# An attention stage whose side work is placed by groups of exponentials, with the gate as a tanh, finer division and the inverse norms as a power on POOL

## Chip, cores and metric

The kernel runs on one core of one Trainium2 chip, in one launch. The metric is device microseconds of one execution. The version before the change had a median of 1349.65 us over three runs.

## What is computed

Input x is [4 batches, 1024 positions, 128 features], float32. Four layers are applied one after the other, each as x = x + layer(layernorm(x)): a selective scan, a mixture of experts, the layer that this text is about, and the mixture of experts again. In the third layer (16 heads of 8 features):

```
sq, sk, sv = lin(x, Wsq), lin(x, Wsk), lin(x, Wsv)      # [T, head, 8]
g = exp(-softplus(lin(x, Wg)))                          # one gate per head = sigmoid(-lin)
M_t = g_t * M_{t-1} + k_t (outer) v_t                   # 8x8 state per head, over 1024 positions
h_t = q_t . M_t                                         # "retention" output, 128 wide
Q, K, V = lin(h, Wq), lin(h, Wk), lin(x, Wv)
Q, K = Q / max(|Q|, 1e-12), K / max(|K|, 1e-12)         # per head, 8 features
attn = softmax(Q K^T * softplus(temp));  out = lin(attn V, Wo)
```

## The kernel before

The stage `attention` (lines 1477 to 2011) runs full softmax attention for all four batches. A **tile** is 128 keys by 512 queries of one head. PE makes its scores (L1605) into PSUM (`att_s_ps`, two buffers of 3 and 2 tiles), ACT takes the exponential of a whole buffer in one instruction (L1770: groups of 3 and 2 tiles in turn, 410 groups in all) into a ring of 15 tiles (`att_prob`), and PE multiplies them with the values (L1620, into `att_o_ps`). Four tiles, one for each of four heads, are one **value step** v; there are 64 of them in a batch, 256 in all. The 410 groups split into 102, 102, 103 and 103 for the four batches.

While PE, DVE, ACT and POOL serve the attention of batch n - 1, the same engines prepare queries, keys and values of batch n. These pieces are the **guests**. They exist during the first three batches only (below: guest batches); batch 0 was prepared by earlier stages, and the fourth has no guest. All guests share one PSUM bank, `att_b_ps`, so they form one chain PE, DVE, PE, DVE. In the order of one guest batch: transpose x and take layernorm statistics; transpose the result; eight products ("make": keys, gate, queries, values, for either half of the positions); 16 units (PE product L1652, DVE outer product L1867, DVE scan L1878, POOL product L1575); two sums over heads (L1693); four projections to Q and K (L1707) with a bias (L1889), a square on POOL (L1581) and a reduction (L1894); the clip (L1898); the inverse norm; four scaled units (L1914); four transposes (L1716), each cut into two half-precision parts (L1921, L1923). SP then copies these parts (`hv_part`) into `att_q_st` and `att_k_st` for the next batch's scores.

The order of each engine is written out by hand. Every engine walks the same list of positions; PE, for each group e, issues the scores of e, then the value step whose exponentials were group e - 2 or earlier, and, only in groups that complete a value step (`closes(e)`, 5 groups of 8), the guest of that value step u. So a guest's place is counted in value steps, 64 to a batch, and DVE and POOL loop over value steps.

The gate: PE makes the product in `att_b_ps`; ACT takes its exponential straight from PSUM (L1758, at u = 13 and 17, behind the exponentials of that group), and PE's next product waits for that; DVE adds 1 (L1857) and takes the reciprocal in two pieces of 256 columns (L1862). The inverse norm: ACT takes the square root of all 256 sums (L1763, u = 53), DVE the reciprocal (L1902). ACT's square root and its exponential stand in different function tables.

The softmax division of batch n - 1 (reciprocal L1807 and product L1809, four pieces of 256 columns) runs in value steps 5, 7, 9 and 11 of the following batch, and for the last batch behind the end of the attention.

Of the kernel before, what the change touches and what calls it, by code (L numbers as in the profile page):

```python
# [112 lines left out]
def load_constants(t, whole):  # L113
# [17 lines left out]
    t.bg_neg = whole.sb("bg_neg", [P, 1])  # L131
# [7 lines left out]
    with Stage(nc, "load") as s:  # L139
# [6 lines left out]
        with nc.Block() as block:  # L146
# [36 lines left out]
            def _(dve):  # L183
# [10 lines left out]
                dve.tensor_scalar(t.bg_neg[:, :], t.col("bg"), -1.0, None, ALU.mult)  # L194
                dve.tensor_scalar(t.bsk_small[:, :], t.col("bsk"), 1.0 / WS, None, ALU.mult)
# [1281 lines left out]
def attention(t):  # L1477
# [30 lines left out]
    def guest(v):  # L1508
        n, u = divmod(v, W)
        return (n + 1, u) if n + 1 < B else (None, None)  # L1510

    def unit_at(u):
        return [w for w in range(UNITS) if 20 + 3 * w // 2 == u]

    with Stage(nc, "att") as q:
# [12 lines left out]
        ss, rn, rt = q.sb("ss", [P, 4, NT * H]), q.sb("rn", [P, 4, NT * H]), q.sb("rt", [P, 2, NT * H])  # L1528
        unit = qm[:, 0:4, :].rearrange("p i (a c) -> p i a c", c=P)
# [9 lines left out]
        inverted, normed = q.count("inverted", 4), q.count("normed", 4)  # L1539
# [5 lines left out]
        made, copied, gated = q.count("made", 8), q.count("copied", 6), q.count("gated", 2)  # L1545
        opened, gate_made = q.count("opened", 2), q.count("gate_made", 4)
# [3 lines left out]
        clipped, rooted, rn_done, scaled = (q.count(n) for n in ("clipped", "rooted", "rn_done", "scaled"))  # L1550
# [4 lines left out]
        with nc.Block() as block:  # L1555

            @block.gpsimd
            def _(pool):
                pool.memset(va[:, :, :, :, HD:32], 1.0).then_inc(blank, 1)
# [8 lines left out]
                def weigh(n, w):  # L1568
                    h, m = divmod(w, HD)
                    pool.wait_ge(scanned.sem, scanned.at(n - 1, w))  # L1570
                    if m == 0:
                        pool.wait_ge(copied.sem, copied.at(n - 1, 3 * h + 1))
# [11 lines left out]
                for v in range(V):  # L1584
                    n, u = guest(v)
                    if u in TURN_X_AT:
                        deviation(n, TURN_X_AT.index(u))
                    if u in PROJECT_QK_AT:
                        square(n, PROJECT_QK_AT.index(u))
                    for w in unit_at(u):  # L1590
                        weigh(n, w)

            @block.tensor
            def _(pe):
# [29 lines left out]
                def project(i, h):  # L1624
                    pe.wait_ge(normed.sem, normed.at(i, 2 * h + 1))
# [48 lines left out]
                def key_value(n, w):  # L1674
                    h, m = divmod(w, HD)
                    if w == 0:
                        pe.wait_ge(copied.sem, copied.at(n - 1, 5))
# [41 lines left out]
                def entertain(n, u):  # L1719
                    if u in TURN_X_AT:  # L1720
                        turn_x(n, TURN_X_AT.index(u))
                    if u in TURN_Z_AT:
                        turn_z(n, TURN_Z_AT.index(u))
                    if u in range(MAKE_AT, MAKE_AT + 8):
                        make(n, u - MAKE_AT)
                    for w in unit_at(u):
                        key_value(n, w)
                    if u in SUM_AT:
                        add_heads(n, SUM_AT.index(u))
                    if u in PROJECT_QK_AT:  # L1730
                        project_qk(n, PROJECT_QK_AT.index(u))
                    if u in TURN_QK_AT:
                        turn_qk(n, TURN_QK_AT.index(u))

                done = 0
                for e in range(GROUPS + BEHIND):
# [5 lines left out]
                    if e < GROUPS and closes(e):  # L1742
# [3 lines left out]
                        n, u = guest(v)  # L1746
                        if n:
                            entertain(n, u)
# [4 lines left out]
            def _(act):  # L1753
                act.sem_inc(exped.sem, exped.start)

                def gate(n, h):
                    act.wait_ge(made.sem, made.at(n - 1, 4 * h + 1))
                    act.activation(g_sb[:, HALVES[h]], b_ps[:, :], ACT.Exp, bias=t.col("bg"),  # L1758
                                   scale=1.0 / WS).then_inc(gated.sem, 1)

                def root(n):
                    act.wait_ge(clipped.sem, clipped.at(n - 1))
                    act.activation(rn[:, :, :], ss[:, :, :], ACT.Sqrt).then_inc(rooted.sem, 1)  # L1763

                for e in range(GROUPS):
# [6 lines left out]
                    if closes(e):  # L1772
                        n, u = guest(first // GH)
                        if u in (MAKE_AT + 2, MAKE_AT + 6):
                            gate(n, (u - MAKE_AT) // 4)
                        if u == ROOT_AT:
                            root(n)

            @block.vector
            def _(dve):  # L1780
# [20 lines left out]
                def divide(i, k):  # L1801
                    cols = slice(k * 256, (k + 1) * 256)
                    if k == 0:
                        dve.wait_ge(moved, (i + 1) * G * MOVES)
                    if k == 2:
# [64 lines left out]
                def scan(n, w):  # L1870
                    h, m = divmod(w, HD)
                    if m == 0:
                        dve.wait_ge(gate_made.sem, gate_made.at(n - 1, 2 * h + 1))
# [52 lines left out]
                def entertain(n, u):  # L1926
                    if u in TURN_X_AT:
                        statistics(n, TURN_X_AT.index(u))
                    if u in NORMAL_AT:
                        normalise(n, NORMAL_AT.index(u))  # L1930
                    if u in TURN_Z_AT:
                        take_z(n, TURN_Z_AT.index(u))
                    if u in range(MAKE_AT, MAKE_AT + 8):
# [215 lines left out]
```

## Time and profile before

| quantity | value |
|---|---|
| three runs | 1346.37, 1349.65, 1355.12 us (median 1349.65) |
| profiled execution | 1350.3 us, of which span 1348.5 us |
| mean granted TensorE clock | 0.926 |
| PE busy | 1086.2 us (81%) |
| ACT busy | 955.5 us (71%) |
| DVE busy | 815.1 us (60%) |
| POOL busy | 344.2 us (26%) |

Busy times are of the whole program; PE is the matmul array, PEld its weight loads. The attention stage reaches from about 577 to 1183 us of the span. A busy PE means that its queue held a running matmul, and in the table nothing is said of who waited for whom; that is read stage by stage.

### The profile page before, as it was taken

The numbers are of one execution on the slowest core, as the hardware profiler recorded it, in microseconds if no ns is written. First come the engines' busy times: TensorE is split into PE (matmuls) and PEld (weight loads), VectorE is DVE, ScalarE is ACT, GpSimd is POOL, SyncE is SP. The second block draws the span as 40 slices with busy tenths as digits, with TensorE's granted clock in tenths as the row PEclk, the third lists the DMA queues.
The fourth block names the chain that finished last, engine by engine and source line by source line (L and its number), as shares of the span: only waits on it lengthen the run. The fifth ranks groups of instructions, "written<-read, shape, count | busy, mean of one in ns | idle before, by whom it ended". The sixth has DMA issues, their size and how long they took to land. (4 is left out here: it accounts for less than half of the span.)

```text
span 1348.5 us, 16297 instructions
## 1 busy us (share of the span) xinstructions
PE 1086.2 (81%) x5850; PEld 384.9 (29%) x5850; DVE 815.1 (60%) x1141; ACT 955.5 (71%) x908; POOL 344.2 (26%) x230
## 2 busy tenths in 40 slices
PE   4647788777699985568997889888997888679996
PEld 3212333233344432212222212222221111134443
DVE  6679999999467747534753666345753300356664
ACT  4667656655388862167888877887878999558885
POOL 3026867668111103210330023100330000011110
PEclk9877999999799997779998999899998999879999
DMA  3001010000101100010101011010110111001112
GB/s 99 10 1 46 32 59 35 32 31 32 32 32 32 32 1 0 1 32 11 24 18 25 21 24 24 9 36 8 24 23 18 31 25 31 8 32 32 32 33 62
DMA packets 24208, 36.73 MB, mean 27 GB/s; under 512 B 7362, under 2 KB 11970, under 8 KB 24130
## 3 DMA queue, kind: packets, MB, share of 16 engines
q1 hardware_dynamic: 24130, 35.71, 9.8%
q8 instruction: 46, 0.75, 0.2%
q14 instruction: 32, 0.26, 0.1%
HBM read 16.82 MB, written 6.29 MB: 17 GB/s over the span
## 5 line engine op out<-in xcount | busy, mean ns | idle before, releaser
L1770 ACT ACTIVATE att_prob<-att_s_ps 128x1536 f32<-128x1536 f32 (+1 forms) x410 | 478.7, 1246 | 95.7 <-PE att_s_ps L1605 95.1
L1620 PE MATMUL att_o_ps<-att_prob,att_va 128*32 128x512 f32 x2048 | 281.9, 623 | 0.0
L1605 PE MATMUL att_s_ps<-att_q_st,att_k_st 32*128 32x512 f16 x1024 | 158.6, 395 | 55.9 <-ACT att_prob L1770 39.0
L734 POOL TENSOR_TENSOR scan_hc<-scan_state,scan_c_rep 128x1024 f32<-128x1024 f32 x64 | 152.5, 2400 | 69.1 <-DVE scan_state L691 68.9
L691 DVE TENSOR_TENSOR_SCAN scan_state<-scan_decay,scan_drive_ps 128x1024 f32<-128x1024 f32 x64 | 143.3, 2271 | 1.1 <-POOL scan_hc L734 1.1
L341 PE MATMUL scan_y_ps<-scan_hc,all_ident 128*128 128x512 f32 x256 | 127.6, 623 | 8.9 <-DVE scan_y_sb L710 6.5
L669 ACT ACTIVATE scan_c_rep<-scan_c_ps 128x1024 f32<-128x1024 f32 x64 | 65.4, 1022 | 83.6 <-PE scan_c_ps L341 83.5
L1605 PEld LDWEIGHTS att_s_ps<-att_q_st,att_k_st 32*128 32x128 f16 x1024 | 37.4, 91 | 285.9 <-ACT att_prob L1770 212.3
L1575 POOL TENSOR_TENSOR att_qm<-att_mem,att_q_sb 128x512 f32<-128x512 f32 x48 | 61.1, 1276 | 203.5 <-DVE att_mem L1878 184.6
L1057 DVE SCALAR_TENSOR_TENSOR ffn_hid_lo<-ffn_hid,ffn_share,ffn_hid_hi 128x1024 f16<-128x1024 f32 x64 | 81.9, 1283 | 49.3 <-ACT ffn_hid_hi L966 48.8
L684 DVE TENSOR_TENSOR scan_drive_ps<-scan_drive_ps,ssm_du_t 128x1024 f32<-128x1024 f32 x64 | 77.3, 1220 | 13.7 <-PE scan_drive_ps L341 13.6
L962 ACT ACTIVATE ffn_hid<-ffn_h_ps,ffn_be 128x1024 f32<-128x1024 f32 x64 | 71.1, 1111 | 20.0 <-PE ffn_h_ps L351 18.6
L1799 DVE COPY att_o_sb<-att_o_ps 128x512 f32<-128x512 f32 x32 | 21.4, 670 | 100.5 <-PE att_o_ps L1620 100.4
L341 PE MATMUL scan_drive_ps<-ssm_bc,ssm_sel 96*128 96x512 bf16 x128 | 41.9, 411 | 49.8 <-DVE scan_state L691 39.3
L351 PE MATMUL ffn_o_ps<-ffn_hid_hi,ffn_w_sel 128*128 128x512 f16 x256 | 75.9, 379 | 2.2 <-DVE ffn_hid_lo L1057 2.2
L966 ACT ACTIVATE ffn_hid_hi<-ffn_hid,ffn_share 128x1024 f16<-128x1024 f32 x64 | 73.5, 1149 | 5.9
L351 PE MATMUL ffn_h_ps<-ffn_z_hi,ffn_w_sel 128*128 128x512 f16 x256 | 76.2, 379 | 0.0
L665 ACT ACTIVATE scan_decay<-ssm_dt_t,all_a_neg 128x1024 f32<-128x1024 f32 x64 | 72.9, 1140 | 0.0
L836 POOL TENSOR_TENSOR ffn_veps<-ffn_mv,all_eps 128x4 f32<-128x4 f32 x16 | 5.1, 319 | 265.0 <-DVE ffn_mv L989 265.0
L847 POOL TENSOR_TENSOR all_x_t<-all_x_t,ffn_y 128x1024 f32<-128x1024 f32 x8 | 24.1, 3007 | 171.4 <-DVE ffn_y L1051 171.4
L341 PEld LDWEIGHTS scan_y_ps<-scan_hc,all_ident 128*128 128x128 f32 x256 | 49.9, 197 | 54.0 <-issue 41.7
L1057 DVE SCALAR_TENSOR_TENSOR ffn_hid_lo<-ffn_hid,all_blend,ffn_hid_hi 128x1024 f16<-128x1024 f32 x32 | 42.6, 1330 | 37.2 <-ACT ffn_hid_hi L966 36.9
(264 smaller groups left out, 1623.7 us busy)
## 6 DMA issues: line engine op xcount, KB each, us to landing
ffn_w_sel<-w_split SPq DMA_DIRECT2D x16, 512.0 KB, 3.2
w_split<-scan_w_parts SPq DMA_DIRECT2D x8, 512.0 KB, 2.9
att_q_st<-hv_part SPq DMA_DIRECT2D x64, 64.0 KB, 2.1
att_k_st<-hv_part SPq DMA_DIRECT2D x64, 64.0 KB, 2.1
ln_x_half<-in_x SPq DMA_DIRECT2D x8, 256.0 KB, 3.0
scan_w_raw<-in_w1e SPq DMA_DIRECT2D x8, 256.0 KB, 3.3
scan_w_raw<-in_w2e SPq DMA_DIRECT2D x8, 256.0 KB, 3.5
out<-store_out SPq DMA_DIRECT2D x8, 256.0 KB, 2.6
```

Source lines behind the costliest of these rows:

```text
L341: last = pe.matmul(out[:, h], w, rhs[:, h], start=start, stop=stop)
L351: last = pe.matmul(out[:, h], w, x[:, h], start=start and i == 0, stop=stop and i == len(parts) - 1)
L665: act.activation(decay[:, n % 4, :], t.dt_t[batches[b]][:, :], ACT.Exp, scale=t.a_neg[:, n:n + 1]).then_inc(decayed.sem, 1)
L684: dve.tensor_tensor(drive_ps[n % 2][:, :], drive_ps[n % 2][:, :], t.du_t[batches[b + n // NS]][:, :], ALU.mult).then_inc(driven.sem, 1)
L691: dve.tensor_tensor_scan(state[:, k % 2, :], decay[:, k % 4, :], drive_ps[k % 2][:, :], 0.0, ALU.mult, ALU.add).then_inc(scanned.sem, 1)
L734: pool.tensor_tensor(hc[:, n % 4, :], state[:, n % 2, :], c_rep[:, n % 4, :], ALU.mult).then_inc(weighed.sem, 1)
L962: act.activation(hid[:, m % 2, :], h_ps[m % 2][:, :], ACT.Gelu_apprx_tanh, bias=b1, scale=1.0 / WS).then_inc(gelued.sem, 1)
L966: act.activation(hid_hi[:, m % 3, :], hid[:, m % 2, :], ACT.Copy, scale=weight_of_expert(k)).then_inc(casted.sem, 1)
L1057: dve.scalar_tensor_tensor(hid_lo[:, m % 3, :], hid[:, m % 2, :], weight_of_expert(m % M // FC), hid_hi[:, m % 3, :], ALU.mult, ALU.subtra ...
L1605: last = pe.matmul(s_ps[e % 2][:, k, :], k_st[rows, g % 2, kc * P:(kc + 1) * P], q_st[rows, g % 2, HALVES[half]], start=True, stop=True)
L1620: last = pe.matmul(o_ps[half][32 * j:32 * j + 32, :], va[:, g % 2, kc, j, :], prob[:, (GH * v + j) % RING, :], start=kc == 0, stop=kc == K ...
L1770: act.activation(prob[:, first % RING:first % RING + k, :], s_ps[e % 2][:, 0:k, :], ACT.Exp).then_inc(exped.sem, 1)
```

## The change

1. A guest's place is counted in groups of exponentials x (102 to a batch) and no longer in value steps u (64 to a batch). Guests may stand in any group, whether it completes a value step or not. DVE and POOL loop over groups too; what belongs to the attention itself on DVE stays at `closes(e)`. All places are new.
2. The gate: DVE copies the product out of PSUM into `g_sb` (a new instruction for each half), which frees the bank; ACT takes a tanh in place in `g_sb` with scale -1/2, three groups later; DVE makes 0.5 * tanh + 0.5 of it. This is sigmoid(-y) as before. The add of 1 and the four reciprocals of a batch are gone.
3. The division of a batch is cut in eight pieces of 128 columns at value steps 5 to 12, before in four of 256 at 5, 7, 9, 11.
4. The inverse norm is one POOL instruction on 128x256, sums to the power -0.5, in place of ACT's square root and DVE's reciprocal. Its exponent comes from a new buffer, `minus_half`, set by POOL ahead of the stage. The places: clip at x = 82, power at 83, DVE's product with the temperature at 85, scaled units at 86 and 87, transposes at 88, 90, 92 and 94.

The core of the diff:

```
-    DIVIDE_AT, PROJECT_AT = (5, 7, 9, 11), (12, 14)
-    TURN_X_AT, NORMAL_AT, TURN_Z_AT = (0, 6), (2, 8), (4, 10)
-    MAKE_AT = 11
+    PIECES = 8
+    DIVIDE_AT, PROJECT_AT = range(5, 5 + PIECES), (12, 14)
+    TURN_X_AT, NORMAL_AT, TURN_Z_AT = (0, 7), (3, 10), (5, 12)
+    MAKE_AT = range(14, 30, 2)
+    GATE_AT, OPEN_AT = (19, 27), (22, 30)
     UNITS = 2 * HD
-    OPEN_AT, INVERT_AT = (16, 19), ((17, 18), (22, 25))
-    SUM_AT = (34, 45)
-    PROJECT_QK_AT = (37, 40, 47, 48)
-    REDUCE_AT = (39, 42, 49, 50)
-    ROOT_AT, RECIPROCAL_AT, UNIT_AT, TURN_QK_AT = 53, 54, (55, 55, 56, 56), (56, 57, 58, 59)
+    UNIT_AT = tuple(31 + 5 * w // 2 for w in range(10)) + (57, 59, 63, 65, 69, 71)
+    SUM_AT = (55, 75)
+    PROJECT_QK_AT = (61, 67, 77, 79)
+    REDUCE_AT = (64, 70, 80, 82)
+    ROOT_AT, RECIPROCAL_AT, SCALE_AT, TURN_QK_AT = 83, 85, (86, 86, 87, 87), (88, 90, 92, 94)
...
-    def guest(v):
-        n, u = divmod(v, W)
-        return (n + 1, u) if n + 1 < B else (None, None)
-
-    def unit_at(u):
-        return [w for w in range(UNITS) if 20 + 3 * w // 2 == u]
+    OPENING = [group_of(GH * W * n) for n in range(B)]
+
+    def guest(e):
+        n = max(i for i in range(B) if OPENING[i] <= e)
+        return (n + 1, e - OPENING[n]) if n + 1 < B else (None, None)
...
+                def root(n):
+                    pool.wait_ge(clipped.sem, clipped.at(n - 1))
+                    pool.tensor_tensor(rn[:, :, :].rearrange("p i c -> p (i c)"), ss[:, :, :].rearrange("p i c -> p (i c)"),
+                                       minus_half[:, :], ALU.pow).then_inc(rooted.sem, 1)
...
                     if p == 0:
                         pe.wait_ge(z_rest.sem, z_rest.at(n - 1, 1))
-                    elif x == 2:
-                        pe.wait_ge(gated.sem, gated.at(n - 1, h))
                     else:
-                        pe.wait_ge(copied.sem, copied.at(n - 1, {4: 2, 1: 0, 3: 1, 5: 3, 7: 4}[p]))
+                        pe.wait_ge(copied.sem, copied.at(n - 1, p - 1))
...
                 def gate(n, h):
-                    act.wait_ge(made.sem, made.at(n - 1, 4 * h + 1))
-                    act.activation(g_sb[:, HALVES[h]], b_ps[:, :], ACT.Exp, bias=t.col("bg"),
-                                   scale=1.0 / WS).then_inc(gated.sem, 1)
-
-                def root(n):
-                    act.wait_ge(clipped.sem, clipped.at(n - 1))
-                    act.activation(rn[:, :, :], ss[:, :, :], ACT.Sqrt).then_inc(rooted.sem, 1)
+                    act.wait_ge(copied.sem, copied.at(n - 1, 4 * h + 1))
+                    act.activation(g_sb[:, HALVES[h]], g_sb[:, HALVES[h]], ACT.Tanh, bias=t.bg_half[:, 0:1],
+                                   scale=-0.5 / WS).then_inc(gated.sem, 1)
...
-                    if x == 1:
-                        return
+                    elif x == 1:
+                        dve.tensor_copy(g_sb[:, HALVES[h]], b_ps[:, :]).then_inc(copied.sem, 1)
...
-                    dve.tensor_scalar(g_sb[:, HALVES[h]], g_sb[:, HALVES[h]], 1.0, None, ALU.add).then_inc(opened.sem, 1)
-
-                def invert_gate(n, h, k):
-                    dve.wait_ge(opened.sem, opened.at(n - 1, h))
-                    cols = slice(h * HALF + k * 256, h * HALF + (k + 1) * 256)
-                    dve.reciprocal(g_sb[:, cols], g_sb[:, cols]).then_inc(gate_made.sem, 1)
+                    dve.tensor_scalar(g_sb[:, HALVES[h]], g_sb[:, HALVES[h]], 0.5, 0.5, ALU.mult,
+                                      ALU.add).then_inc(opened.sem, 1)
...
                 def reciprocals(n):
                     dve.wait_ge(rooted.sem, rooted.at(n - 1))
-                    dve.reciprocal(rn[:, :, :], rn[:, :, :]).then_inc(rn_done.sem, 1)
-                    dve.wait_ge(rn_done.sem, rn_done.at(n - 1))
```

## Rows read from the trace of the kernel before

**Rows 1.** Busy time by engine, three guest batches, then the batch without guests; columns named.

```profile
core 0: us, PE busy (x) PEld busy (x) DVE busy (x) ACT busy (x) POOL busy (x), PEclk, DMA share, GB/s
584.84:737.66 152.82, 133.57 (x940) 34.49 (x943) 75.06 (x108) 124.13 (x107) 26.96 (x24) 0.94 0.09 19
737.66:892.46 154.80, 134.94 (x961) 34.74 (x964) 84.33 (x120) 124.31 (x108) 26.88 (x24) 0.97 0.10 21
892.46:1047.99 155.53, 134.96 (x963) 34.84 (x965) 84.38 (x120) 125.79 (x108) 26.89 (x24) 0.97 0.10 21
1047.99:1165.80 117.81, 102.82 (x778) 20.47 (x778) 16.16 (x21) 116.92 (x103) 0.00 (x0) 1.00 0.12 24
```

**Rows 2.** The same view, third guest batch cut at x = 14, 31, 55, 83.

```profile
909.99:940.23 30.24, 24.46 (x176) 7.02 (x180) 15.09 (x22) 21.56 (x21) 0.33 (x1) 1.00 0.03 7
940.23:972.50 32.27, 30.28 (x214) 6.60 (x216) 25.80 (x27) 28.20 (x25) 10.20 (x8) 1.00 0.12 26
972.50:1015.31 42.81, 39.22 (x296) 11.28 (x294) 23.66 (x31) 33.14 (x28) 14.28 (x12) 1.00 0.11 22
1015.31:1047.99 32.68, 24.25 (x166) 5.97 (x170) 10.74 (x16) 26.68 (x24) 0.00 (x0) 0.90 0.10 22
```

**Rows 3.** Stretches x = 14 to 31 and from 83 on, first and second guest batch.

```profile
602.70:632.60 29.90, 24.32 (x176) 6.65 (x168) 8.18 (x12) 21.72 (x20) 0.00 (x0) 0.94 0.00 1
707.90:737.66 29.76, 22.92 (x160) 5.78 (x160) 10.74 (x16) 25.12 (x23) 0.00 (x0) 0.89 0.11 24
...
754.47:785.73 31.26, 26.57 (x183) 6.93 (x175) 16.15 (x25) 21.66 (x20) 0.12 (x1) 0.95 0.02 3
860.39:892.46 32.07, 23.70 (x164) 5.78 (x160) 10.74 (x16) 25.14 (x24) 0.00 (x0) 0.89 0.10 23
```

**Rows 4.** PE's order of time at a gate: start, length, work, idle before and releaser.

```profile
924.86 0.39 PE L1652 MATMUL att_b_ps<-att_z_hi,all_ret_hi 128*128 128x512 f16 x1 [2.13 <-ACT att_g_sb L1758]
```

**Rows 5.** ACT's order of time around the square root, third guest batch.

```profile
1011.73 8.29 ACT L1770 ACTIVATE att_prob<-att_s_ps 128x1536 f32<-128x1536 f32 x7 [0.30 <-PE att_s_ps L1605]
1020.03 1.28 ACT L1763 ACT_TABLE_LOAD   x1
...
1023.06 4.62 ACT L1770 ACTIVATE att_prob<-att_s_ps 128x1024 f32<-128x1024 f32 x4
```

**Rows 6.** PE's order of time behind the same square root.

```profile
1024.13 0.39 PE L1605 MATMUL att_s_ps<-att_q_st,att_k_st 32*128 32x512 f16 x2 [2.68 <-ACT att_prob L1770]
```

**Rows 7.** Busy time by engine in the stretch behind it (columns as in rows 1).

```profile
1025.47:1034.00 8.53, 8.53 (x44) 2.12 (x45) 2.37 (x4) 5.71 (x5) 0.00 (x0) 0.60 0.00 0
```

**Rows 8.** Groups of instructions in the stage: count, busy us, mean ns, idle before.

```profile
L1862 DVE RECIPROCAL att_g_sb<-att_g_sb 128x256 f32<-128x256 f32 x12 | 20.8, 1733 | 0.0
```

**Rows 9.** The same view, POOL's instructions.

```profile
L1575 POOL TENSOR_TENSOR att_qm<-att_mem,att_q_sb 128x512 f32<-128x512 f32 x48 | 61.1, 1276 | 203.5 <-DVE att_mem L1878 184.6 <-PE att_b_ps L1693 19.0
L1565 POOL TENSOR_TENSOR att_rstd<-att_veps,all_minus_half 128x4 f32<-128x4 f32 x6 | 6.0, 1008 | 0.5
L1563 POOL TENSOR_TENSOR att_veps<-att_mv,all_eps 128x4 f32<-128x4 f32 x6 | 1.2, 200 | 117.5 <-DVE att_mv L1822 117.5
```

**Rows 10.** The last projection on PE, in order of time.

```profile
1008.88 1.16 PE L1707 MATMUL att_b_ps<-all_qk_mats,hv_h_seq 128*128 128x128 f32 x8 [0.46 <-DVE att_raw L1889]
```

**Rows 11.** DVE's order of time from the clip to the first scaled unit.

```profile
1012.95 0.29 DVE L1898 TENSOR_SCALAR att_ss<-att_ss 128x256 f32<-128x256 f32 x1
...
1023.56 0.36 DVE L1906 TENSOR_TENSOR att_rt<-att_rn,all_heat 128x64 f32<-128x64 f32 x2
1023.96 0.69 DVE L1914 TENSOR_TENSOR att_qm<-att_raw,att_rt 128x512 f32<-128x512 f32 x1
```

**Rows 12.** ACT's order of time at the start of the last stage, behind the exponentials.

```profile
1193.36 0.20 ACT L948 ACTIVATE ffn_th<-ffn_gap 1x1 f32<-1x1 f32 x1 [1.44 <-DVE ffn_gap L1015]
1193.58 1.28 ACT L962 ACT_TABLE_LOAD   x1
```

**Rows 13.** One transpose of a scaled unit on PE, in order of time.

```profile
1038.86 0.66 PE L1716 MATMUL att_b_ps<-all_ident,att_qm 128*128 128x128 f32 x4
```

More of the change, by code:

```diff
@@ L1549, in attention @@
         qk_made, raw_done, squared, sums = (q.count(n, 4) for n in ("qk_made", "raw_done", "squared", "sums"))
-        clipped, rooted, rn_done, scaled = (q.count(n) for n in ("clipped", "rooted", "rn_done", "scaled"))
+        clipped, rooted, scaled = (q.count(n) for n in ("clipped", "rooted", "scaled"))
         unit_done, qk_turned, hi_done, lo_done = (q.count(n, 4) for n in ("unit_done", "qk_turned", "hi_done", "lo_done"))
@@ L1582, in square @@
                                        ALU.mult).then_inc(squared.sem, 1)
[L1584 to L1591, printed above, removed]
+                def root(n):
+                    pool.wait_ge(clipped.sem, clipped.at(n - 1))
+                    pool.tensor_tensor(rn[:, :, :].rearrange("p i c -> p (i c)"), ss[:, :, :].rearrange("p i c -> p (i c)"),
+                                       minus_half[:, :], ALU.pow).then_inc(rooted.sem, 1)
+                for e in range(GROUPS):
+                    n, x = guest(e)
+                    if x == ROOT_AT:
+                        root(n)
+                    if x in TURN_X_AT:
+                        deviation(n, TURN_X_AT.index(x))
+                    if x in UNIT_AT:
+                        weigh(n, UNIT_AT.index(x))
+                    if x in PROJECT_QK_AT:
+                        square(n, PROJECT_QK_AT.index(x))
             @block.tensor
@@ L1717, in turn_qk, with entertain @@
                     last.then_inc(qk_turned.sem, 1)
[L1719 to L1733, printed above, removed]
+                def entertain(n, x):
+                    if x in TURN_X_AT:
+                        turn_x(n, TURN_X_AT.index(x))
+                    if x in TURN_Z_AT:
+                        turn_z(n, TURN_Z_AT.index(x))
+                    if x in MAKE_AT:
+                        make(n, MAKE_AT.index(x))
+                    if x in UNIT_AT:
+                        key_value(n, UNIT_AT.index(x))
+                    if x in SUM_AT:
+                        add_heads(n, SUM_AT.index(x))
+                    if x in PROJECT_QK_AT:
+                        project_qk(n, PROJECT_QK_AT.index(x))
+                    if x in TURN_QK_AT:
+                        turn_qk(n, TURN_QK_AT.index(x))
                 done = 0
@@ L1771, in _ @@
                                    ACT.Exp).then_inc(exped.sem, 1)
[L1772 to L1777, printed above, removed]
+                    n, x = guest(e)
+                    if x in GATE_AT:
+                        gate(n, GATE_AT.index(x))
             @block.vector
@@ L1924, in take_qk @@
                                       ALU.subtract).then_inc(lo_done.sem, 1)
[L1926 to L1933, printed above, removed]
-                        take(n, u - MAKE_AT)
-                    if u in OPEN_AT:
-                        open_gate(n, OPEN_AT.index(u))
-                    for h in range(2):
-                        if u in INVERT_AT[h]:
-                            invert_gate(n, h, INVERT_AT[h].index(u))
-                    for w in unit_at(u):
-                        outer(n, w)
-                        scan(n, w)
-                    if u in SUM_AT:
-                        take_sum(n, SUM_AT.index(u))
-                    if u in PROJECT_QK_AT:
-                        add_bias(n, PROJECT_QK_AT.index(u))
-                    if u in REDUCE_AT:
-                        reduce(n, REDUCE_AT.index(u))
-                    if u == RECIPROCAL_AT:
@@ new lines, in entertain @@
+                def entertain(n, x):
+                    if x in TURN_X_AT:
+                        statistics(n, TURN_X_AT.index(x))
+                    if x in NORMAL_AT:
+                        normalise(n, NORMAL_AT.index(x))
+                    if x in TURN_Z_AT:
+                        take_z(n, TURN_Z_AT.index(x))
+                    if x in MAKE_AT:
+                        take(n, MAKE_AT.index(x))
+                    if x in OPEN_AT:
+                        open_gate(n, OPEN_AT.index(x))
+                    if x in UNIT_AT:
+                        outer(n, UNIT_AT.index(x))
+                        scan(n, UNIT_AT.index(x))
+                    if x in SUM_AT:
+                        take_sum(n, SUM_AT.index(x))
+                    if x in PROJECT_QK_AT:
+                        add_bias(n, PROJECT_QK_AT.index(x))
+                    if x in REDUCE_AT:
+                        reduce(n, REDUCE_AT.index(x))
+                    if x == RECIPROCAL_AT:
@@ L1950, in entertain @@
                         reciprocals(n)
                     for i in range(4):
[L1952 removed]
+                        if x == SCALE_AT[i]:
                             make_unit(n, i)
[L1954 to L1955 removed]
+                    if x in TURN_QK_AT:
+                        take_qk(n, TURN_QK_AT.index(x))
                 for g in range(2):
                     take_values(g)
[L1959 to L1970 removed]
+                for e in range(GROUPS):
+                    if closes(e):
+                        v = tiles_of(e)[0] // GH
+                        if v >= KC + 2 and (v - 3) % KC == KC - 1:
+                            g, half = divmod((v - 3) // KC, 2)
+                            take_out(g, half)
+                            if half == 1 and g + 2 < B * G:
+                                take_values(g + 2)
+                        if v >= W:
+                            if v % W in DIVIDE_AT:
+                                divide(v // W - 1, DIVIDE_AT.index(v % W))
+                            if v % W in PROJECT_AT:
+                                add_out(v // W - 1, PROJECT_AT.index(v % W))
+                    n, x = guest(e)
@@ L1971, in _ @@
                     if n:
-                        entertain(n, u)
+                        entertain(n, x)
                 take_out(B * G - 1, 1)
-                for k in range(4):
+                for k in range(PIECES):
                     divide(B - 1, k)
```

43 lines of the change are left out of this document (16 added, 27 removed).

## The prediction

> **What bounds the kernel now.** All that changes lies in the attention stage, so I read it alone, cut at the first exponential of each batch [rows 1]. The fourth batch, without guests, takes 117.81 us; ACT is busy for 116.92 of them, so there ACT is the bound, at 117.81 / 103 = 1.144 us a group. PE is at 102.82 / 117.81 = 87%. The guest batches take 152.82, 154.80 and 155.53 us: 36.1, 38.1 and 37.7 us more than 102 or 103 groups at that pace. ACT falls to 81%, PE stands at 87%. What the reader is to see: guests make PE's queue late, scores come late and ACT waits. Hence a guest costs either its own work on PE, or a wait at which PE stands with the scores behind it.
>
> Cutting the third guest batch by the new positions x [rows 2] tells the two apart. From x = 31 to 55 PE is busy for 30.28 of 32.27 us, 94%, with the clock at 1.00: nothing but work. From 55 to 83 it is 92%. From 14 to 31 (products and gates) it is 24.46 of 30.24 us, 81%, for 17 groups that would take 19.4 without guests. From 83 on (root, units, transposes) it is 24.25 of 32.68 us, 74%, at a mean clock of 0.90, for 20 groups worth 22.9. These two stretches hold the waits. The two other guest batches show the same [rows 3]: 29.90 and 31.26 us, 29.76 and 32.07 us.
>
> **The products and the gate (x = 14 to 31).** At a gate PE stands still for 2.13 us until ACT has emptied the bank, behind the exponentials of that group [rows 4]; two gates in a batch. In the new order ACT reads no bank: DVE copies, PE goes on two groups later. A DVE pass over 512 columns takes 0.69 us (the scaled unit, [rows 11]), so PE finds the bank free after two groups (2.3 us), and ACT's tanh, three groups after the copy's place, finds its input. What is queued behind each wait: behind PE's wait for the copy the next scores, behind ACT's wait for it the exponentials, behind DVE's wait for the tanh, three groups on, its next take and its copies of finished output. All three have two or three groups of room. The two stalls are 4.3 us, and a guest in every second group instead of in every value step spreads the rest. I do not book both in full: I let PE reach the 94% of the next stretch. The PE work of 24.32, 26.57 and 24.46 us then takes 25.9, 28.3 and 26.1 us; against 29.90, 31.26 and 30.24 this saves 4.0, 3.0 and 4.1. The second one holds a stretch at less than full clock (0.95) that should go with the stall, 1.5 us more. Mean 4.2 us a batch. DVE loses twelve reciprocals, 20.8 us [rows 8], and gains six copies of 0.69; it is at 54% here [rows 1], so this is worth only what it takes out of the chain, which is in the 94%.
>
> **Units, sums, projections (31 to 83).** Ten units stand in 24 groups as before; I book nothing to x = 55. From 55 to 83 PE goes from 92 to 94%: 39.22 / 0.938 = 41.8 against 42.81, 1.0 us. The tightest new wait is the second sum at 75, four groups (4.6 us) behind the last unit at 71, whose PE product, outer product, scan and POOL product (1.28 [rows 9]) come to about 4 us. It may cost some tenths either way.
>
> **Square root to power (83 on).** The exponentials end at 1020.02 and start again at 1023.06: 3.04 us, of which one table load is 1.28 [rows 5]. PE waits 2.68 us for that [rows 6], and then comes what the busy shares hide: for 8.53 us from 1025.47 the granted clock is 0.60 on average [rows 7], that is mostly at 1.2 instead of 2.4 GHz. The transposes fall into that stretch. The excess over 1.144 us a group from x = 83 on is 8.0, 10.3 and 9.8 us [rows 2, 3], mean 9.4. With the root off ACT 3.1 of them go. Of the remaining 6.3 I keep 1.4 at the end of the batch, where the next scores wait for their copies, and 1.9 for four transposes of 0.66 us [rows 13], of which part fits in PE's spare 13%. So 3.0 more goes with the half clock, and the saving is 6.1 us a batch. On the table loads the Trainium skill ("ScalarE: Activation LUTs", What ACT_TABLE_LOAD costs) adds about 1.38 us of drain to each load of 1.28, so some 5.3 us for the pair; the trace shows no drain, the load starts 0.01 us after the last exponential [rows 5]. By the page the sum would be about 7 us lower; the measurement decides.
>
> **The power's own price** is the open term: POOL, 128x256. The trace has only 128x4, 1.008 us, beside 0.200 for an add of that size and 1.276 for a multiply of 128x512 [rows 9]. Lower bound: all that the power adds is paid once, and further elements cost what a multiply's do, (1.276 - 0.200) / 508 = 2.1 ns: 1.008 + 0.53 = 1.5 us. Upper bound: all of it is paid for each element, 0.202 us: 0.200 + 256 x 0.202 = 51.9 us. For the forecast I scale it like the multiply, from 4 to 256 elements 0.734 / 0.200 = 3.7 times: 3.7 us. The multiply is the one POOL operation with both sizes here, and for it nearly all of the small instruction is a fixed part. The Trainium skill ("GPSIMD Engine Reference", Performance versus the Vector engine) gives about 2.6 cycles an element for two-input work and no price for a power; by it alone the whole instruction would be under 1 us, below my lower bound, which the 1.008 us for four elements contradicts. How much is free? From the start of the last projection on PE (1008.88 [rows 10]) to the end of the clip (1013.24 [rows 11]) passed 4.4 us. That projection now stands at x = 79, the first transpose at 88: nine groups, 10.3 us, and about 0.9 for guests between. Behind the power come the temperature product and the first unit, 1.1 us (1023.56 to 1024.65 [rows 11]). 11.2 - 4.4 - 1.1 leaves 5.7 us. At 3.7 the power is hidden; the cover is those five groups. Beyond 5.7 us PE waits at the first transpose with all scores behind it, and DVE waits with its output copy behind it.
>
> **The rest.** Eight pieces of division: hidden in the batches, where shorter pieces help a little, but exposed at the very end: eight more DVE instructions. Their fixed part is between nothing and 0.18 us, the length of an instruction of 64 columns [rows 11], so 0 to 1.4 us; I take 1.0 as each also waits for the one before it. The setting of the exponent, 256 columns on POOL, is a few tenths of a microsecond ahead of the stage, while the first scores wait for their copies: nothing. The half bias is one DVE instruction of one column during loading: nothing.
>
> **Sum.** 4.2 + 1.0 + 6.1 = 11.3 us a guest batch, 33.9 for three, less 1.0: 32.9. 1350.3 - 32.9 = 1317.4 us of the profiled execution, which stood 0.65 over the median: **1317 us**. Own range 1303 to 1331: PE at 97% through the three middle stretches (about 3.3 us a batch) and no wait for copies (1.4) give 1303; half the gain of the product stretch (2.1) and transposes that keep 2.1 more give 1331.
>
> **Rivals.**
> *A, the power is long.* For: it adds 0.8 us for four elements, four times the add, and no row has it at size. Against: the multiply's fixed part. PE stalls for X - 5.7 in each guest batch, and a stalled PE falls to half clock as after the root, so the 3.0 are lost too. All gains are eaten at X = 5.7 + 11.3 - 3.0 - 0.3 (the end) = 13.7 us; it is over 1% (13.5 us, about what this measurement can tell from no change) slower from 18.2 on. The geometric mean of 3.7 and 51.9 is 13.9, which gives no change, 1350. In full (51.9) it is 46.2 + 3.0 - 11.3 = 37.9 a batch, 1463 us.
> *B, placement buys nothing.* PE has work for 135 us in each guest batch [rows 1]; waits for DVE could take the place of the waits for ACT in the one chain through the bank. Then only x = 83 on gains: 18 - 1 = 17 us, 1333. Against it: the 2.13 us waits are on ACT, which in the new order holds no bank.
> *C, the tanh brings table loads.* Two of 1.28 at each of six gates, 15.4 us, 1333. Against: in the last stage a tanh follows the exponentials with no load before it, and the load comes only for the next function [rows 12].
>
> **Chances.** Forecast 0.50; B 0.13; A between 5.7 and 18 us 0.19, beyond 0.15; C 0.03. Faster by over 1% are the forecast nearly whole, over half of B and C, and A up to about 9.2 us: 0.61. Slower by over 1% is A beyond 18: 0.17. The rest, 0.22, is within 1%. The range goes from 1303 to 1372, where A stands at about 21 us; this leaves out about 5% below and 13% above.
>
> **What the profile will show.** ACT: no table load in the stage but the first, no pause before x = 88. PE: no wait for the gate; busy share from x = 14 to 31 at about 94%, clock 1.00 behind x = 83. POOL: three powers of 128x256; under 5.7 us I am right, near 14 or more rival A. A wait of PE for DVE at the places of the copies would be B. Guest batches of about 143 us instead of 154. I am wrong if the power is long, or if the half clock has another cause than that pause.

## The result and the profile after

The changed kernel takes 1407.92 us (median of 4 runs, 1401.16 to 1409.08) against 1351.96 us for the one before: 1.041 times as long, 95% interval 1.036 to 1.046. The forecast was 1317 us in a range to 1372; the sign was wrong. The profiled execution took 1407.79 us, its span 1406.0.

First the busy times by engine in the three guest batches and the last batch, cut at the same exponentials as [rows 1].

```profile
core 0: us, PE busy (x) PEld busy (x) DVE busy (x) ACT busy (x) POOL busy (x), PEclk, DMA share, GB/s
587.99:761.00 173.01, 133.43 (x941) 34.52 (x945) 66.70 (x105) 120.66 (x105) 68.13 (x25) 0.86 0.08 17
761.00:931.51 170.51, 130.88 (x961) 34.26 (x963) 77.76 (x125) 120.11 (x104) 68.17 (x25) 0.89 0.09 19
931.51:1104.94 173.43, 133.05 (x967) 34.59 (x966) 77.65 (x125) 121.60 (x105) 68.17 (x25) 0.89 0.09 19
1104.94:1222.35 117.41, 102.08 (x774) 20.42 (x770) 17.05 (x29) 116.82 (x104) 0.00 (x0) 1.00 0.12 24
```

POOL's busy time in a guest batch rose from 26.9 to 68.2 us, by 41.3; nothing else grew. Each guest batch is 16 to 20 us longer, 53.8 in all. The batch without guests is as before. Of the other 3.7 us of the span, 3.2 lie ahead of the first exponential (588.0 against 584.8); the first exponential of the later runs came anywhere from 579.8 to 587.7, with either code, so that is variation. 1.0 lies behind the last exponential.

The same view cut at x = 14, 31, 55 and 83, third guest batch, answers to [rows 2].

```profile
949.18:974.00 24.82, 24.46 (x177) 6.46 (x176) 15.74 (x27) 21.32 (x20) 0.00 (x0) 1.00 0.02 4
974.00:1004.70 30.70, 30.28 (x214) 6.78 (x218) 20.14 (x21) 28.27 (x25) 10.20 (x8) 1.00 0.13 26
1004.70:1043.82 39.12, 38.09 (x288) 10.93 (x280) 21.52 (x29) 32.71 (x29) 15.15 (x13) 1.00 0.11 22
1043.82:1104.94 61.12, 24.36 (x170) 6.14 (x170) 8.90 (x15) 23.06 (x21) 40.41 (x1) 0.69 0.07 14
```

Three stretches are shorter than before, by 5.4, 1.6 and 3.7 us here, with PE at 97 to 99%. The last is 28.4 us longer, with one POOL instruction in it. The order of time of that place, one fence for each engine (DVE, POOL, PE, ACT), answers to [rows 5, 6, 11].

```profile
1042.62 0.30 DVE L1897 TENSOR_SCALAR att_ss<-att_ss 128x256 f32<-128x256 f32 x1
1084.27 0.36 DVE L1903 TENSOR_TENSOR att_rt<-att_rn,all_heat 128x64 f32<-128x64 f32 x2 [41.35 <-POOL att_rn L1590]
1084.66 0.69 DVE L1911 TENSOR_TENSOR att_qm<-att_raw,att_rt 128x512 f32<-128x512 f32 x1
```

```profile
1042.99 41.24 POOL L1590 TENSOR_TENSOR att_rn<-att_ss,att_minus_half 128x256 f32<-128x256 f32 x1 [1.28 <-DVE att_ss L1897]
```

```profile
1048.91 1.06 PE L1631 MATMUL att_o_ps<-att_prob,att_va 128*32 128x512 f32 x8
1085.41 1.12 PE L1725 MATMUL att_b_ps<-all_ident,att_qm 128*128 128x128 f32 x4 [35.44 <-DVE att_qm L1911]
1086.46 1.03 PE L1616 MATMUL att_s_ps<-att_q_st,att_k_st 32*128 32x512 f16 x5
1087.42 1.94 PE L1631 MATMUL att_o_ps<-att_prob,att_va 128*32 128x512 f32 x8
...
1091.15 1.07 PE L1631 MATMUL att_o_ps<-att_prob,att_va 128*32 128x512 f32 x8
```

```profile
1040.24 10.54 ACT L1776 ACTIVATE att_prob<-att_s_ps 128x1536 f32<-128x1536 f32 x9 [0.25 <-PE att_s_ps L1616]
1087.11 2.37 ACT L1776 ACTIVATE att_prob<-att_s_ps 128x1024 f32<-128x1024 f32 x2 [36.32 <-PE att_s_ps L1616]
```

The power takes 41.24 us. DVE's next instruction waits for it, PE's first transpose waits for DVE, the scores stand behind that transpose, and ACT has nothing for 36.32 us. After it the transpose takes 1.12 us and eight value products 1.94, where they take 0.66 [rows 13] and 1.07: PE's clock has halved, for some 5 us. The gates are clean: ACT's tanh follows its exponentials with no table load and no wait (third guest batch; one of the two gates is shown).

```profile
953.64 3.31 ACT L1776 ACTIVATE att_prob<-att_s_ps 128x1024 f32<-128x1024 f32 x3 [0.61 <-PE att_s_ps L1616]
956.85 0.71 ACT L1768 ACTIVATE att_g_sb<-att_g_sb,all_bg_half 128x512 f32<-128x512 f32 x1
957.46 2.35 ACT L1776 ACTIVATE att_prob<-att_s_ps 128x1536 f32<-128x1536 f32 x2
```

### The profile page after: what moved, and what is told of

It reads as the page before. It is cut to its first block and busy times, and to the rows that moved or that the text cites. A ratio compares the mean times of both kernels' runs of the same rounds, so it can differ in the third digit from the quotient of the medians.

```text
span 1406.0 us, 16315 instructions
## 1 busy us (share of the span) xinstructions
PE 1084.1 (77%) x5850; PEld 386.8 (28%) x5850; DVE 795.2 (57%) x1165; ACT 943.1 (67%) x899; POOL 467.5 (33%) x234
## 5 line engine op out<-in xcount | busy, mean ns | idle before, releaser
L1631 PE MATMUL att_o_ps<-att_prob,att_va 128*32 128x512 f32 x2048 | 278.7, 617 | 0.0
L1616 PE MATMUL att_s_ps<-att_q_st,att_k_st 32*128 32x512 f16 x1024 | 157.4, 393 | 38.0 <-ACT att_prob L1776 27.2
L342 PE MATMUL scan_y_ps<-scan_hc,all_ident 128*128 128x512 f32 x256 | 130.6, 637 | 8.6 <-DVE scan_y_sb L711 6.5
L1590 POOL TENSOR_TENSOR att_rn<-att_ss,att_minus_half 128x256 f32<-128x256 f32 x3 | 123.7, 41240 | 3.8 <-DVE att_ss L1897 3.8
L1725 PE MATMUL att_b_ps<-all_ident,att_qm 128*128 128x128 f32 x48 | 10.1, 346 | 106.1 <-DVE att_qm L1911 106.0
```

The costliest lines, as they stand in the source:

```text
L342: last = pe.matmul(out[:, h], w, rhs[:, h], start=start, stop=stop)
L1590: pool.tensor_tensor(rn[:, :, :].rearrange("p i c -> p (i c)"), ss[:, :, :].rearrange("p i c -> p (i c)"), minus_half[:, :], ALU.pow).then ...
L1616: last = pe.matmul(s_ps[e % 2][:, k, :], k_st[rows, g % 2, kc * P:(kc + 1) * P], q_st[rows, g % 2, HALVES[half]], start=True, stop=True)
L1631: last = pe.matmul(o_ps[half][32 * j:32 * j + 32, :], va[:, g % 2, kc, j, :], prob[:, (GH * v + j) % RING, :], start=kc == 0, stop=kc == K ...
```

## The experiments

Every figure of a stretch below is the mean over the three guest batches of the time between the starts of two exponentials, in us. "Newton" is the run with the inverse norm on DVE, the base of several others. The code excerpts are shortened: slices, waits and semaphores are left out where they only follow from the line shown.

| run | 0-14 | 14-31 | 31-55 | 55-83 | from 83 | median | ratio to before (95%) |
|---|---|---|---|---|---|---|---|
| before | 17.4 | 30.5 | 32.4 | 42.7 | 31.5 | 1352 | |
| changed | 17.7 | 24.0 | 30.5 | 39.1 | 61.1 | 1407.9 | 1.041 (1.036 to 1.046) |
| root back | 17.7 | 24.0 | 30.5 | 39.1 | 28.1 | 1303.0 | 0.966 (0.962 to 0.970) |
| power alone | 18.7 | 30.0 | 32.4 | 42.7 | 60.4 | 1437.1 | 1.065 (1.060 to 1.069) |
| Newton | 17.7 | 24.0 | 30.5 | 39.1 | 23.1 | 1292.6 | 0.958 (0.954 to 0.962) |
| gate alone | 17.4 | 27.0 | 32.1 | 42.7 | 31.2 | 1339.5 | 0.991 (0.988 to 0.995) |
| gate back (on Newton) | 17.7 | 29.1 | 30.5 | 39.1 | 23.1 | 1303.5 | 0.967 (0.963 to 0.971) |
| four pieces (on Newton) | 17.7 | 24.0 | 30.5 | 39.1 | 23.1 | 1288.2 | 0.953 (0.950 to 0.957) |
| no table load (on before) | 17.8 | 31.0 | 32.4 | 42.7 | 26.1 | 1337.9 | 0.989 (0.986 to 0.993) |
| quarter power (on changed) | 18.2 | 24.0 | 30.5 | 39.1 | 29.9 | 1312.8 | 0.971 (0.965 to 0.977) |
| units in pairs (on Newton) | 17.7 | 24.0 | 32.3 | 38.8 | 23.1 | 1290.2 (one run) | |
| price by size (on before) | 17.4 | 31.0 | 32.4 | 42.7 | 30.6 | 1353.2 (one run) | |

The last run changes nothing in the guest batches, so it is a second trace of the kernel before: against the first it differs by 0.5 us from 14 to 31 and by 0.9 from 83. What is read from one pair of traces in these two columns is no surer than that, where the code of before is one of the pair.

**The root back.** Only the inverse norm undone in the changed kernel.

```
-    pool.tensor_tensor(rn, ss, minus_half, ALU.pow).then_inc(rooted.sem, 1)         # POOL, x = 83
+    act.activation(rn[:, :, :], ss[:, :, :], ACT.Sqrt).then_inc(rooted.sem, 1)      # ACT, x = 83
+    dve.reciprocal(rn[:, :, :], rn[:, :, :]).then_inc(rn_done.sem, 1)               # DVE, x = 85
```

> The changed kernel with the inverse norm as it was before: ACT's square root at x = 83, DVE's reciprocal at x = 85; all else changed. Theory 1 (the power alone makes the change slow, the rest gains): the stretches before x = 83 keep what they gained in the changed kernel, 6.5 + 1.9 + 3.6 = 12.0 us a guest batch, and from x = 83 on it is as in the kernel before: 1350 - 36 = about 1314 us, ratio 0.973. Rival (the new placement only looks good because PE comes rested or early out of the stall): 1340 us or more.

Measured: 1303.0 us. The three middle stretches are to a tenth those of the changed kernel, so the gains are not owed to the stall: theory 1, with 11 us more. They came from x = 83 on, 28.1 us where I had left the 31.5 of before; the spread places help there too.

**The power alone.** The same edit the other way round, in the kernel before, at u = 53 and 54.

> The kernel before with only the inverse norm as one POOL power of 128x256, places as they were. Theory 1: it takes 41.2 us from the clip's end (1013.24 in the third guest batch of the trace before), the first unit is ready 1.1 us later at about 1055.6, while PE came to the first transpose at 1027.75: 28 us more in each guest batch, about 1434 us, ratio 1.062; that is worse than the change as a whole. Rival (the long power comes only with the new places, by contention with other work): under 1380 us, and a power well under 41 us.

Measured: 1437.1 us. In the old places the power takes the same time.

```profile
L1588 POOL TENSOR_TENSOR att_rn<-att_ss,att_minus_half 128x256 f32<-128x256 f32 x3 | 123.7, 41244 | 4.0 <-DVE att_ss L1901 4.0
```

It alone costs 86 us, the change as a whole 56: the rest of the change wins, and this hid in the result.

**The price by size.** Seven POOL instructions more in the fourth batch of the kernel before, on a buffer whose first operand is 2.5 and whose second is -0.5 everywhere.

```
+    for size, op in ((4, ALU.pow), (16, ALU.pow), (64, ALU.pow), (128, ALU.pow), (16, ALU.mult), (64, ALU.mult), (256, ALU.mult)):
+        pool.tensor_tensor(probe[:, 2, 0:size], probe[:, 0, 0:size], probe[:, 1, 0:size], op).then_inc(probed, 1)
```

> The kernel before with seven instructions more on POOL during the fourth batch, where POOL has nothing else: powers of 128x4, 128x16, 128x64 and 128x128, multiplies of 128x16, 128x64 and 128x256, each waiting for the one before it; nobody waits for them, so the time stays at 1350 us. If the power pays for each element, (41.24 - 1.01) / 252 = 0.160 us each: 1.0, 2.9, 10.6 and 20.8 us. If it pays by blocks or only with this data: steps in that row, or another slope. The multiplies: 0.2 to 0.75 us.

Measured: 1353.2 us in one run, against 1350 expected. POOL's groups of instructions in that batch (sizes 16 and 64 hold a power and a multiply each):

```profile
L1603 POOL TENSOR_TENSOR att_probe<-att_probe 128x128 f32<-128x128 f32 x1 | 20.8, 20780 | 0.1
L1603 POOL TENSOR_TENSOR att_probe<-att_probe 128x64 f32<-128x64 f32 x2 | 10.9, 5433 | 0.2
L1603 POOL TENSOR_TENSOR att_probe<-att_probe 128x16 f32<-128x16 f32 x2 | 3.1, 1560 | 0.2
L1603 POOL TENSOR_TENSOR att_probe<-att_probe 128x4 f32<-128x4 f32 x1 | 1.0, 1007 | 0.1
L1603 POOL TENSOR_TENSOR att_probe<-att_probe 128x256 f32<-128x256 f32 x1 | 0.7, 734 | 0.1
```

The last is the multiply of 256: 0.734 us, what the interpolation in the prediction gave. The power is a straight line: (20.78 - 1.007) / 124 = 0.159 us for each element of a partition, and about 0.4 fixed; and from here to the norms' 256 elements, which hold other values, the slope is the same, (41.24 - 20.78) / 128 = 0.160. So at four elements 0.6 of the 1.0 us was already payment by the element.

**Newton on DVE.** A first guess from the bits and three Newton steps in place of POOL's power.

```
+    sh = ss_bits >> 1;  guess_bits = 0x5f3759df - sh          # two tensor_scalar on 128x256
+    3 x: tm = y * y;  tm = (tm * -0.5) * ss;  y = (tm + 1.5) * y
```

> The changed kernel with the inverse norm on DVE alone: a first guess of the inverse root by shift and subtraction on the bits, then three Newton steps, eleven short instructions of 128x256 instead of POOL's power. Theory 1: about 0.3 to 0.4 us each, some 4 us in all, under the 5 to 6 us that are free; the stall of 36.3 us and the half clock behind it go from each guest batch: 1408 - 3 x (36.3 + 2) = about 1293 us, ratio 0.957 to the kernel before. Rival (half clock behind x = 83 has another cause than a pause of PE): the granted clock falls there all the same, and the time is 1300 us or more.

Measured: 1292.6 us, 4.2% under the kernel before. The eleven instructions take 4.8 us (DVE's order of time, the first and the last of them):

```profile
959.85 0.29 DVE L1895 TENSOR_SCALAR att_sh<-att_ss 128x256 uint32<-128x256 uint32 x1
...
964.19 0.43 DVE L1901 SCALAR_TENSOR_TENSOR att_rn<-att_tm,att_rn 128x256 f32<-128x256 f32 x1
```

The cover (the time for which the norm may take and delay nobody, 5.8 us) hides them: PE has no wait at its first transpose. From x = 83 on the stretch takes 23.6 us for 20 groups, 0.7 over the pace of the batch without guests, with the clock at full.

```profile
960.73:984.35 23.62, 22.10 (x170) 5.63 (x170) 12.56 (x24) 23.06 (x21) 0.00 (x0) 1.00 0.17 36
```

**The gate alone**, in the kernel before (copy, tanh, 0.5 t + 0.5 as in the diff of the change, places in value steps), and **the gate back**, in the run with Newton:

```
-    dve.tensor_copy(g_sb[...], b_ps[:, :])                                            # x = 16, 24
-    act.activation(g_sb[...], g_sb[...], ACT.Tanh, bias=t.bg_half, scale=-0.5 / WS)   # x = 19, 27
+    act.activation(g_sb[...], b_ps[:, :], ACT.Exp, bias=t.col("bg"), scale=1.0 / WS)  # x = 18, 26
+    # + 1 at x = 22, 30; four reciprocals at x = 24, 26, 35, 40; make(n, 2) waits for gated
```

> The kernel before with only the new gate: copy out of PSUM by DVE, tanh in place one value step later, 0.5 t + 0.5, no reciprocals of the gate; places in value steps, square root and four division pieces as before. Theory G (the gate's waits were most of what the stretch x = 14 to 31 gained, 6.5 us a guest batch): that stretch falls from about 30.5 to about 26 us, 1350 - 14 = about 1336 us. Rival P (the new places gained it): the stretch stays at 29 us or more, 1345 us.

> The run with the Newton norm, with the gate as it was: exponential straight from PSUM, plus 1, four reciprocals a batch; all new places and the eight pieces kept. Theory G: the two waits of about 2 us come back in each guest batch and the stretch x = 14 to 31 goes from about 24 to 28 us: 1293 + 13 = about 1306 us. Rival P: 1297 us or less.

Measured: 1339.5 and 1303.5 us. The stretch from 14 to 31 goes from 30.5 to 27.0 by the gate alone and from 24.0 to 29.1 when it is taken back. Theory G holds in both; the gate is worth 3.4 us a guest batch in the old places and 5.1 in the new ones. The places alone bring 1.4 with the old gate and 3.1 with the new one: each is worth more with the other. The wait is back in the second run, and the clock over that stretch stands at 0.94, where the run with Newton has 1.00 (third guest batch):

```profile
PE att_b_ps L1656 <- ACT att_g_sb L1763: 3.7, 2, 1.8
```

```profile
877.45:906.85 29.40, 25.73 (x178) 6.90 (x177) 17.86 (x27) 21.58 (x19) 0.00 (x0) 0.94 0.02 4
```

**Four pieces** (`PIECES = 4`, at 5, 7, 9, 11, in the run with Newton).

> The run with the Newton norm, with the division in four pieces of 256 columns as before. If the shorter pieces free the chain through DVE in the stretch x = 0 to 31, some 0.5 us a guest batch comes back, and the end is shorter by about 1 us: between 1291 and 1294 us, no difference that can be measured. A rise of 5 us or more would say that the pieces were a main part of the gain.

Measured: 1288.2 us, all stretches as with eight pieces (24.0 us each from 14 to 31), and 182.9 us from the end of the last exponential to the end of the program against 183.3 us. Over all traces this last part takes 182.5 to 183.0 us with four pieces (six traces) and 183.3 to 183.8 with eight (six traces): the division in eight pieces brings nothing in the batches and costs about 0.9 us at the end. The 4.4 us between the two medians are not explained by it: the intervals of the two ratios overlap, and the two profiled executions took 1287.5 and 1286.9 us.

**No table load** (`ACT.Copy` in place of `ACT.Sqrt`, in the kernel before).

> The kernel before with a plain copy in place of ACT's square root, so that no function table is changed; the norms are then the reciprocal of the sums, not of their roots, and the output is another one. Theory 2 (the pause of ACT stops PE, and the half clock is the pause's doing): the pause of 3.04 us shrinks to about 0.4, PE's wait goes, the clock stays at 1.00 through the transposes: 3 x (2.6 + about 3) = 17 us less, about 1334 us. Rival (the half clock comes from the sparse work of this stretch): the clock falls all the same, 3 x 2.6 = 8 us less, about 1342 us.

Measured: 1337.9 us. The three stretches from x = 83 on stand at 1.00, 0.98 and 1.00 (before: 0.89, 0.89, 0.90).

```profile
1010.26:1037.07 26.81, 21.14 (x166) 5.56 (x170) 10.67 (x16) 23.57 (x22) 0.00 (x0) 1.00 0.12 27
859.30:886.21 26.91, 21.14 (x164) 5.37 (x160) 10.74 (x16) 22.24 (x22) 0.00 (x0) 0.98 0.13 28
711.91:736.55 24.64, 20.31 (x160) 5.39 (x160) 10.65 (x16) 22.01 (x21) 0.00 (x0) 1.00 0.13 29
```

They are 5.4 us shorter than before in the mean: 2.6 of table loads, and a rest of 2.8 that went with the half clock (4.4 and 1.9 against the second trace of before). That rest is a difference, not a row: the two waits of PE left in the stretch, 1.3 us for DVE's half-precision parts and 0.8 to 2.5 for the copies, are the same as before. The median lies between the two forecasts, but the clock is theory 2's: without PE's pause it does not fall at the transposes, with the same work in the stretch.

**A quarter of the power**, in the changed kernel.

```
-    pool.tensor_tensor(rn, ss, minus_half, ALU.pow).then_inc(rooted.sem, 1)
+    pool.memset(rn[:, 64:256], 0.001)
+    pool.tensor_tensor(rn[:, 0:64], ss[:, 0:64], minus_half[:, 0:64], ALU.pow).then_inc(rooted.sem, 1)
```

> The changed kernel with POOL's power on 64 of the 256 columns only; the others are set to a constant, so that three quarters of the norms are not computed. Theory 3 (a power of any length is free up to about 5.8 us, beyond that PE stands still for the rest, and then the half clock costs about 2.6 us more): 10.5 + 0.3 us on POOL, PE waits 5 us, 3 x (5.0 + 2.6) = 23 us over the run with the Newton norm (1293): about 1316 us. Rival (part of the stall is absorbed, or the cover is not what the places say): under 1303 us, or over 1325.

Measured: 1312.8 us. Third guest batch, POOL's order of time, PE's waits, and the busy times of the 5 us behind the stall:

```profile
975.50 10.54 POOL L1592 TENSOR_TENSOR att_rn<-att_ss,att_minus_half 128x64 f32<-128x64 f32 x1
```

```profile
PE att_b_ps L1726 <- DVE att_qm L1912: 4.9, 1, 4.9
```

```profile
987.00:992.00 5.00, 4.78 (x21) 1.75 (x21) 3.26 (x6) 2.37 (x2) 0.00 (x0) 0.50 0.00 0
```

10.54 + 0.3 of setting less 4.9 leaves 5.9 us free; at full length it is 41.24 - 35.44 = 5.8. In the mean of the three batches the stretch is 6.8 us over that with Newton: 4.8 of wait, and 2.0 more that go with the half clock. Theory 3, with the clock's share 0.6 smaller than expected.

**Units in pairs.** The places of the first ten units.

```
-    UNIT_AT = tuple(31 + 5 * w // 2 for w in range(10)) + ...     # 31, 33, 36, 38, 41, ...
+    UNIT_AT = (31, 32, 36, 37, 41, 42, 46, 47, 51, 52) + ...
```

> The run with the Newton norm, with the first ten units in pairs of neighbouring groups, x = 31, 32, 36, 37 and so on to 52, in place of every second or third group; the count of units in the stretch x = 31 to 55 is the same. A unit keeps DVE for about 2.1 us (0.74 + 1.36) and a group lasts 1.14. Theory 4 (even spacing took PE's waits for DVE out of this stretch): PE's weight loads wait for DVE's outer product again, five times 0.5 to 1 us, and the stretch goes from 30.7 to 33 us or more, as in the kernel before (32.3) or over it. Rival (the stretch gained because DVE lost the reciprocals of the gate, or because guests may stand beside any group): it stays within 0.5 us of 30.7.

Measured: 32.9, 32.2 and 31.7 us for that stretch, mean 32.3 where even spacing has 30.5 and the kernel before 32.4. PE's weight loads wait for DVE again; the first row is of this run, the second of the kernel before, same stretch of the third guest batch. The run with Newton has no such row in the third batch, and in the first two it has 2.5 and 1.7 us in three and two waits, where this run has five in each.

```profile
PEld att_b_ps L1656 <- DVE att_z_tok L1859: 4.2, 5, 0.8
```

```profile
PEld att_b_ps L1652 <- DVE att_z_tok L1867: 3.3, 4, 0.8
```

The loss, 2.7, 1.5 and 1.0 us in the three batches, reaches the 33 us of theory 4 in the first batch only, and 0.7 of that came back in the next stretch; but it is beyond the rival's 0.5 in all three, on one trace. So even spacing is the cause, with its size known to about 1 us. Neither the missing reciprocals (the run with the gate back has them at x = 35 and 40 and still 30.5) nor the freedom of the place (these pairs use it too) did it.

## Why the prediction was wrong

**The step that failed** is the power's own price, "For the forecast I scale it like the multiply". It measured 41.24 us where I took 3.7. The time, 1408 us, fell outside the range to 1372, and on the other side of no change. The two bounds held (1.5 and 51.9), and the upper one's rule, payment by the element, was the true one: 0.160 us an element where the row of four elements gave 0.202 with the fixed part in it. What I had for the choice was one size of the power. The reason given for it, that "the multiply is the one POOL operation with both sizes here", misreads [rows 9]: the instruction of four elements is an add, and the multiply stands there at 512 only. As a price of the multiply it came out right all the same; but what it says of the multiply says nothing of the power's loop, and the 0.8 us by which the power exceeds the add could be either. The row could not decide it, and the forecast should have stood on that: rival A had 0.34 in all, its long half 0.15 (0.17 a little further on; the two do not agree).

**What followed from a long power was priced right.** The 5.7 us of cover are 5.8 and 5.9 in two runs. A stalled PE does fall to half clock behind the stall; this costs 2.0 us (quarter power) to 2.7 (full power) where I said 3.0. By rival A's formula a power of 41.2 would give 35.5 + 3.0 - 11.3 = 27.2 us a guest batch, about 1432 us; it came to 1408, as the gains were under-sized.

**The gains**, in us a guest batch:

| stretch | forecast | measured | cause, as the runs show it |
|---|---|---|---|
| 14 to 31 | 4.2 | 6.5 | gate 3.4 (gate alone) to 5.1 (gate back), places the rest |
| 31 to 55 | 0 | 1.8 | even spacing of the units (units in pairs) |
| 55 to 83 | 1.0 | 3.6 | new places (with the gate alone 42.7, as before) |
| from 83, Newton in the power's place | 6.1 | 8.4 | places 3.4 (before against root back), pause and half clock of the root 5.0 (root back against Newton) |
| sum | 11.3 | 20.3 | |

The common error in the middle stretches is the 94%, read as "nothing but work" and used as the ceiling for the others. PE reached 97 to 99%. The missing 6% were waits: from 31 to 55 PE is busy for 30.28 us with 214 matmuls before and after, and only its idle time falls, from 2.0 to 0.4 us. The rows of PE's waits for the kernel before name them, from 31 to 55 of the third guest batch:

```profile
PE att_b_ps L1652 <- DVE att_z_tok L1867: 1.0, 2, 0.5
PE att_s_ps L1605 <- ACT att_prob L1770: 0.9, 4, 0.3
```

So the waits for DVE in the chain through the bank, which rival B feared, were there before and went with the new places: from x = 14 to 83 the matmuls wait for DVE for 4.4 to 5.4 us in each guest batch before, and not once in the changed kernel. Of these, 2.1 to 2.2 us lie in the stretch from 55 to 83, which gained 3.6. What is shown of that stretch is that the new places did it; which of them was not taken apart.

The gates were over-sized in turn. The prediction counted 4.3 us for two waits of 2.13; one row had been looked at. PE's waits in all three guest batches, the first four rows of the kernel before, the last of the run with Newton, say 9.1 us for six, 3.0 a batch:

```profile
PE att_b_ps L1652 <- ACT att_g_sb L1758: 9.1, 6, 2.1
PE att_b_ps L1652 <- DVE att_z_tok L1867: 5.5, 10, 0.8
PE att_s_ps L1605 <- DMA att_k_st<-hv_part: 5.5, 3, 2.5
PE att_b_ps L1716 <- DVE hv_part L1923: 3.8, 3, 1.3
PE att_s_ps L1609 <- DMA att_k_st<-hv_part: 0.4, 2, 0.2
```

The third and fourth row are the places' part of the last stretch: 1.8 us a batch in which the next scores wait for their copies, of which the prediction kept 1.4 as a cost, and 1.3 in which one transpose waits for DVE to take the one before it. With the transposes spread over x = 88 to 94 the second is gone and the first is 0.1.

**The rest.** Six tanh without a table load: rival C falls, as [rows 12] said. Rival B falls: apart from the stall behind the power, no matmul of a guest batch waits for DVE in the changed kernel, and from x = 14 on the weight loads that do wait at most 0.8 us each. The eight pieces: hidden in the batches as said; at the end about 0.9 us, forecast 1.0. The drain of 1.38 us that the Trainium skill ("ScalarE: Activation LUTs", What ACT_TABLE_LOAD costs) adds to a load did not show: ACT's pause of 3.04 us [rows 5] is two loads of 1.28 and the root's own 0.42, which leaves no room for it.

```profile
1020.03 1.28 ACT L1763 ACT_TABLE_LOAD   x1
1021.33 0.42 ACT L1763 ACTIVATE att_rn<-att_ss 128x256 f32<-128x256 f32 x1
1021.76 1.28 ACT L1770 ACT_TABLE_LOAD   x1
```

## What to carry to other kernels

A duration at one small size does not give the price at another, and the size law of a neighbouring operation is no substitute: when an operation moves to an engine where it has run only on a few elements, price both laws, look at which of them the change survives, and measure one larger size first. Two sizes would have been enough. In a chain that all engines serve by turns, space the guests by their slowest link and keep an engine with a deep queue out of the bank that the others need; and do not let PE, which feeds the bound, stand: here 2.7 us of pause were enough for half clock behind it.

## What the runs showed of the hardware

POOL's power costs 0.16 us for each element of a partition, 75 times the multiply's 2.1 ns, on one line through 4, 64, 128 and 256 elements; as DVE work the same inverse norm, by bit guess and three Newton steps, took 4.8 us for 128x256 against 41.24. A pause of PE of 2.7 us was followed by a fall of its clock from 2.4 to 1.2 GHz (0.60 on average over 8.5 us [rows 7]), and without the pause the clock stood at 1.00, 0.98 and 1.00; after pauses of 4.9 and 35.4 us it stood at 0.50 for some 5 us from the restart, so the longer pauses did not make the half clock last longer. The best version found is the changed kernel with the Newton norm; with four pieces of division it took 1288.2 us, 0.953 of the kernel before (0.950 to 0.957), with eight 1292.6 us, and the two can't be told apart.
